# A Mamba block with an fp8 feed-forward on one core: two scalings go from VectorE to ScalarE, and the hand-written step tables of four engines get new places

## The reference, cut to what matters

```python
xz = x @ W_in + b_in;  x_in, z = split(xz)             # 256 inner channels each
x_conv = silu(conv1d(x_in, conv_w, causal, 4 taps) + conv_b)
Bm, Cm = split(x_conv @ W_xp + b_xp)                   # 16 states
delta  = softplus(x_conv @ W_dt + b_dt)
h_t = exp(delta_t * A) * h_{t-1} + (delta_t * x_t) * B_t   # per channel and state
y_t = sum_s h_t[s] * C_t[s] + D_skip * x_t
out = (y * silu(z)) @ W_out + b_out
x1  = x + layernorm(layernorm_alpha_beta(xn + out))    # xn = layernorm(x)
# feed-forward: per-tensor fp8 (e4m3) rounding of both operands
hq, wq = fake_quant_fp8(layernorm(x1)), fake_quant_fp8(weight)
out = x1 + layernorm(hq @ wq.T + bias)
```

## Time and profile before

| what | us |
|---|---|
| median of 3 runs | 593.94 (593.66 to 595.33) |
| the profiled execution | 596.42 |
| its span, first to last instruction | 594.7 |
| busy: PE / DVE / ACT / POOL | 512.0 / 502.9 / 433.9 / 351.0 |

### The profile page before, as it was taken

The page is one execution under the profiler, slowest core; times in us unless marked ns, Lnnn a source line. Parts: engine busy times, 40 slices in busy tenths (PEclk is TensorE's granted clock), DMA queues, the critical chain, the costliest instruction groups (busy, mean ns, idle before and its releaser), DMA issues.

```text
span 594.7 us, 9011 instructions
## 1 busy us (share of the span) xinstructions
PE 512.0 (86%) x2875; PEld 397.1 (67%) x2875; DVE 502.9 (85%) x1013; ACT 433.9 (73%) x870; POOL 351.0 (59%) x327
## 2 busy tenths in 40 slices
PE   6989899998899989997999889988999879765292
PEld 4557686877687767876687758676877668655030
DVE  5167699988998998889898899898789999987786
ACT  2558994999579965999399949995699958730264
POOL 3054364948577674948394858676585759530154
PEclk8989999999899889998899999998999899878555
DMA  7201633053505360434304350535042514460018
GB/s 185 63 1 23 121 69 74 11 98 72 106 2 107 62 115 2 76 62 85 64 15 94 72 107 1 106 73 107 0 89 54 107 35 81 78 127 0 1 35 196
DMA packets 19918, 41.21 MB, mean 69 GB/s; under 512 B 3744, under 2 KB 10016, under 8 KB 19872
## 3 DMA queue, kind: packets, MB, share of 16 engines
q0 software_dynamic: 9936, 34.87, 31.1%
q1 hardware_dynamic: 9936, 5.78, 3.7%
HBM read 3.68 MB, written 2.10 MB: 10 GB/s over the span
## 4 chain that ended last, share of the span: by engine, by line
PE 52%; DVE 20%; ACT 12%; POOL 8%; issue 5%; DMA 0%; DVEq 0%; POOLq 0%; ACTq 0%
PE drive L1078 16%; PE hT L1095 11%; PE fbank L1021 8%; DVE state L1301 8%; PE fbank L1036 4%; PE drive L1075 3%; DVE acc_d L1324 3%; ACT term L828 3%; POOL u L538 3%; PE fbank L1113 2%; ACT nrm L718 2%; PE drive L1021 2%; ACT L771 2%; POOL state L687 1%; PE fbank L1105 1%
## 5 line engine op out<-in xcount | busy, mean ns | idle before, releaser
L1301 DVE TENSOR_TENSOR_SCAN state<-decay,drive 128x512 f32<-128x512 f32 x256 | 297.5, 1203 | 28.2 <-ACT decay L807 12.2
L807 ACT ACTIVATE decay<-delta,a_neg 128x510 f32<-128x510 f32 x256 | 171.3, 729 | 23.8 <-DVE state L1301 22.0
L1095 PE MATMUL hT<-ident,state 128*128 128x128 f32 x1024 | 148.8, 282 | 22.2 <-DVE acc_d L1324 13.8
L1078 PE MATMUL drive<-diag,uT 128*128 128x256 f32 x640 | 165.0, 405 | 0.8 <-DVE uT L1503 0.8
L1095 PEld LDWEIGHTS hT<-ident,state 128*128 128x128 f32 x1024 | 122.9, 146 | 49.5 <-ACT term L828 16.0
L1078 PEld LDWEIGHTS drive<-diag,uT 128*128 128x128 f32 x640 | 125.5, 206 | 20.2 <-issue 3.4
L828 ACT ACTIVATE term<-hT,Ct 128x256 f32<-128x256 f32 x256 | 102.5, 483 | 4.9 <-PE hT L1095 4.9
L550 POOL TENSOR_TENSOR scaled<-uT,Bt 128x1024 f32<-128x1024 f32 x48 | 95.8, 1996 | 5.9 <-DVE uT L1503 4.2
L565 POOL TENSOR_SCALAR_AFFINE_SELECT diag<-Bt 128x512 f32<-128x512 f32 x80 | 59.1, 793 | 35.4 <-PE drive L1078 17.6
L581 POOL DMA_DIRECT2D acc<-term x64 | 61.6, 967 | 18.5 <-issue 9.5
L1324 DVE SCALAR_TENSOR_TENSOR acc_d<-hT,Ct,acc_d 128x256 f32<-128x256 f32 x160 | 66.6, 471 | 5.3 <-PE hT L1095 5.3
(11 more groups left out here) (190 smaller groups left out, 661.6 us busy)
## 6 DMA issues: line engine op xcount, KB each, us to landing
acc<-term POOLq DMA_DIRECT2D x64, 512.0 KB, 4.8
out_dram<-x_all SPq DMA_DIRECT2D x7, 256.0 KB, 3.0
x_all<-term POOLq DMA_DIRECT2D x5, 256.0 KB, 3.9
x_all<-in_L_attn_x_dram SPq DMA_DIRECT2D x2, 256.0 KB, 4.0
state<-in_L_attn_conv_w_dram SPq DMA_DIRECT2D x1, 512.0 KB, 5.9
w_in<-in_L_attn_W_in_dram SPq DMA_DIRECT2D x1, 256.0 KB, 4.7
w_dt<-in_L_attn_W_dt_dram SPq DMA_DIRECT2D x1, 256.0 KB, 4.5
out_dram<-x_all SPq DMA_DIRECT2D x2, 128.0 KB, 2.7
```

What stands on the lines that cost most here:

```text
L807: last = nc.scalar.activation(decay[:, g % DECAYS, h, :, s, 1:], delta[:, par, h, :, 1:], ACT.Exp, scale=a_neg[:, h, SG * g + s:SG * g + s ...
L1078: last = nc.tensor.matmul(dst[:, :, P * c:P * c + P], uT[:, par, TC * b + c, P * h:P * h + P], diag[:, n % DIAGS, c, :, :], start=True, st ...
L1095: last = nc.tensor.transpose(hT[:, ring(n, c), DI * s + P * h:DI * s + P * h + P], state[:, n % STATES, h, s, P * c:P * c + P], ident[:, :])
L1301: nc.vector.tensor_tensor_scan(state[:, n % STATES, h, :, :].rearrange("p s t -> p (s t)"), decay[:, g % DECAYS, h, b, :, :].rearrange("p ...
```

## The change

Four parts. (1) In the feed-forward, ScalarE scales the weight and the bias, behind its first two scalings of h; VectorE keeps the five column instructions. TensorE's first bias product waits for ScalarE's two. (2) `LEAD` is 2, not 3: at unit n GpSimd makes the factor of unit n + 2. (3) The last unit made by a product is 14, not 15. (4) Some twenty places in the four tables move, most of them by one to three.

```diff
-LEAD = 3
+LEAD = 2
-MUL_U = (2, 6, 8, 10, 12, 15)
+MUL_U = (2, 6, 8, 10, 12, 14)
-POOL_STEPS = dict(front_root=(2,), front_residual=(31,), front_u=(25,), back_gate=(9,), back_affine=(18,),
-                  back_sum=(25,), sum_states=(5,), back_root=(15, 22, 25))
-ACT_STEPS = dict(back_h2T=(47,), front_xin=(5, 9), silu_table=(21,), front_silu=(21, 22, 23), exp_table=(23,),
-                 front_norm=(12,), front_xnT=(23,), front_dt=(29, 30), front_exp=(34,), front_log=(34,),
+POOL_STEPS = dict(front_root=(5,), front_residual=(27,), front_u=(25,), back_gate=(10,), back_affine=(20,),
+                  back_sum=(25,), sum_states=(8,), back_root=(15, 22, 25))
+ACT_STEPS = dict(back_h2T=(47,), front_xin=(5, 7), silu_table=(21,), front_silu=(21, 22, 23), exp_table=(23,),
+                 front_norm=(12,), front_xnT=(23,), front_dt=(25, 30), front_exp=(34,), front_log=(34,),
...
-PE_STEPS = dict(front_in=(1, 5, 20, 22), front_transpose=(24,), front_dt=(25, 28), front_bc=(36,),
-                front_ut=(41, 44), back_y=(12, 14), back_out=(18,), back_transpose=(46,))
-DVE_STEPS = dict(front_stats=(1,), front_shift=(4,), front_low=(19,), front_bc=(25,), front_delta=(24,),
+PE_STEPS = dict(front_in=(1, 5, 20, 22), front_transpose=(23,), front_dt=(25, 27), front_bc=(36,),
+                front_ut=(39, 42), back_y=(12, 14), back_out=(18,), back_transpose=(46,))
+DVE_STEPS = dict(front_stats=(1,), front_shift=(5,), front_low=(19,), front_bc=(24,), front_delta=(23,),
...
-        XS_STEPS = 10
+        XS_STEPS = 8
...
+                if grp.v == -1:
+                    act.wait_ge(xs_step, 7)
+                    nc.scalar.activation(wqT_g[:, :], wqT[:, :], ACT.Copy, scale=units[1]).then_inc(units_ready, 1)
+                    nc.scalar.activation(bias_g[:, :], fb_r[:, :], ACT.Copy, scale=units[3]).then_inc(units_ready, 1)
...
-                    pe.wait_ge(xs_step, XS_STEPS)
+                    pe.wait_ge(units_ready, 2)
...
                 nc.vector.tensor_scalar(sg, g, s_, None, ALU.mult).then_inc(xs_step, 1)
-                nc.vector.tensor_scalar(wqT_g[:, :], wqT[:, :], g, None, ALU.mult).then_inc(xs_step, 1)
-                dve.wait_ge(xs_step, 8)
-                nc.vector.tensor_scalar(bias_g[:, :], fb_r[:, :], sg, None, ALU.mult).then_inc(xs_step, 1)
+                dve.wait_ge(xs_step, 7)
                 nc.vector.tensor_scalar(eps, sg, sg, LN_EPS, ALU.mult, ALU.mult).then_inc(xs_step, 1)
```

More of the change, by code:

```diff
@@ L385, in build_sandwich @@
         xs_step = sem("xs_step")
+        units_ready = sem("units_ready")
         t_ready = sem("t_ready")
@@ L406, in build_sandwich @@
         x_k = x_all[:, :].rearrange("p (k d) -> p k d", d=DM)
-        XS_STEPS = 10
+        XS_STEPS = 8
         B_STEPS = 8
+        units = [x_scale[:, k:k + 1] for k in range(3, 8)]
         block = ctx.enter_context(nc.Block())
@@ L1585, in to_units @@
             def to_units():
-                inverse, g, s_, sg, eps = (x_scale[:, k:k + 1] for k in range(3, 8))
+                inverse, g, s_, sg, eps = units
                 nc.vector.tensor_scalar(inverse, x_scale[:, 0:1], wq_scale[:, 0:1], 1.0 / FP8_MAX ** 2,
```

## The result

The changed kernel took 615.48 us in the median of 4 runs (612.52 to 619.03), the kernel before 593.8 us in the runs beside it (592.89 to 595.33): a ratio of 1.0365, with a 95% interval of 1.029 to 1.044. The direction was forecast, the size was not: 21.7 us were lost, not 6.6, and the time lies above the range. A few executions of the experiments lay far off the others of their kernel (853 us in run 9, with TensorE at about half its clock throughout, 1277 in run 8, 625 in run 12, 606 in run 10); the ratios leave them out.

The account below looks back on a forecast made before the run. VectorE was taken to set each slot's end. Terms of 1.4 us per slot made 8.4 in six, less 0.4 in the feed-forward; with all or no clock falls, 604.4 or 599.2, taken as 600.5 us; range 588.5 to 605.

Parts of the forecast that it names:

- Rival B: Rival from the experiments: TensorE's and GpSimd's new order, with the shorter lead, costs the time by itself; no chance given.
- variance -0.45: VectorE's variance in each of six slots: no longer held by GpSimd's masks, 0.62 becomes 0.17 us, 0.45 us gained.
- delta +0.83: VectorE's delta, moved ahead of one scan: held by GpSimd's product, 0.83 us lost in each of six slots.
- shift of piece 4 +1.0: VectorE's shift of norm piece 4: held until GpSimd's u ends, 1.0 us lost per slot, the largest single term.
- VectorE's first rounding: Feed-forward: the rounding starts when GpSimd's first sum is done, 0.05 us behind it, gaining 0.4 us.
- Nothing is held by tensor_tensor: Rival: GpSimd's f32 tensor products hold no VectorE instruction; delta and shift lose nothing, 588 to 591 us; chance 0.27.
- the rival with a free delta: Rival: holds partly covered, delta not held and the clock's falls ending; 0.8 us per slot, 595.6 us; chance 0.11.
- the second hold: Rival: GpSimd's product for unit 12 holds VectorE's shift of piece 2; 2.4 us more per slot, 615; chance 0.08.
- falls that might vanish: TensorE's drops to half clock cost 5.2 us of the profiled execution; between none and all might remain.
- The mask of unit 15: GpSimd, behind the second root: TensorE gets it at about 406, still ahead of VectorE's demand; no cost counted.

Follow-up runs that it names:

- run 9: Kernel before with only GpSimd's part of the change (lead two, unit 14 for 15, GpSimd's steps): 599.78 to 602.24 us, ratio 1.0120.
- run 8: Kernel before with only VectorE's delta, B and C at their changed steps: 597.98 us, ratio 1.0065.
- run 12: Changed kernel with unit 12's product waiting for the shift of piece 2, delta, B, C and TensorE's steps as before: 592.19 us.
- run 10: Changed kernel with GpSimd's part undone (lead three, unit 15 scaled, GpSimd's steps as before): 599.6 us, ratio 1.0092.
- run 6: Changed kernel with one wait more: GpSimd's product for unit 12 waits for VectorE's shift of piece 2; 596.53 us, ratio 1.0036.
- run 14: Changed kernel with GpSimd's product for unit 12 moved ahead of the DMA of unit 5, no wait added: 599.11 us, ratio 1.0077.
- run 1: Changed kernel with ScalarE's first front_dt at step 29 again, not 25: 613.61 us.
- run 3: Changed kernel with ScalarE's first front_dt and VectorE's delta, B and C at their old steps: 608.53 us.
- run 13: Kernel before with only GpSimd's part of the change, profiled once more with TensorE's mean clock at 0.94: 602.18 us in one execution.
- run 4: Kernel before with only ScalarE's scaling of the feed-forward's weight and bias, steps and lead unchanged: 593.22 us, ratio 0.9984.
- run 5: Changed kernel with the lead of three again and unit 15 scaled by GpSimd, not 14: 633.83 us.
- run 7: Changed kernel with unit 12's product waiting for the shift of piece 2, and delta, B and C as before: 589.5 us, ratio 0.9924.
- run 11: Changed kernel, delta, B, C as before; unit 12's product waits for piece 2's shift, unit 15's mask for piece 6's: 586.91 us, ratio 0.9885.

## Why the prediction was right in direction and wrong in size

**The bound was read rightly.** VectorE's closed row sets the slot's end: the period grew by 3.56 us for 3.8 us of holds, with TensorE waiting longer for acc_d (28.5 us in 19 waits, before 13.8 in 14). Rival B of the experiments fell with runs 6 and 14, which keep every other part of the change and lose 2.4 and 5.4 us.

**The three terms of the forecast were right as holds**: variance -0.45 (measured -0.45), delta +0.83 (+0.72), shift of piece 4 +1.0 (+0.93; the forecast's own times, 398.6 to 399.65 less the shift's 0.15, give 0.9), 1.2 us a slot for 1.4. VectorE's first rounding came 0.4 us earlier, as forecast. The Trainium skill's rule ("SBUF — State Buffer", section "SBUF: two separate sides"), by which one of VectorE and GpSimd holds a shared port pair for a whole instruction, is borne out for products of f32: 1.92 us for 1.20, delta's own work beginning about where the product ends, and 1.08 us for 0.15, ending with u. "Nothing is held by tensor_tensor", which had 0.27, is excluded. So is the rival with a free delta (0.11, 595.6): its time lies near run 6's, but delta was held in full there.

**The step that failed** is the one on the second hold: "From the traces the DMA's issue comes too late for it. Chance 0.08." The rival's mechanism and place were right. Its price was too low, 2.4 us a slot where 2.50 + 0.53 were measured, and that its 615 meets 615.48 is luck: it stands on a base of 600.5 where run 6 has 596.53. The prediction gives no times for "too late". Worked out again from the traces, an estimate: ScalarE ended unit 5's term at 382.60 in the kernel before, 0.8 us later is 383.4, and the DMA's row starts 0.6 us behind the term's end (331.49 and 332.10 in the changed kernel), so at 384.0, with the product's row 0.58 us behind it at 384.6 and the shift at 384.27. The rows came out so: DMA 0.18 us ahead of the shift, product 0.40 behind its start. The step's fault is its condition that the product must start "just before" the shift: it took for granted that a product can hold only what starts after its own row does. Runs 6 and 14 show that this was wrong: with the same starts to 0.02 us, the shift is free when the product isn't ready behind the DMA, and held to the product's end when it is. Runs 1, 3 and 13 show a second fault of that step: it asked about one instruction. Three small instructions stand there in a row (L1378, L1380, L1357), the product is longer than all three, and which of them it catches depends on 0.9 us of ScalarE's time. So the chance of a hold there was more than that of one instruction being caught.

By the same page's rule, whoever starts first keeps the pair; the trace agrees only if the start is not that of the product's row. For the shift at 332.28 the rows alone would give it the pair, and it was held.

**The clock.** The forecast took off between 0 and 5.2 us for falls that might vanish, and chose the middle. What happened is another thing: the falls are still there (0.95 in every second period) and cost nothing, 66.45 us against 66.44. Where VectorE's row is longer than TensorE's work, TensorE at half clock has room. So even without the second hold the 600.5 would have been some 4 us too high: run 6, which is the change without it, took 596.53. With the whole of the 5.2 us off, the forecast's terms give 593.94 + 8.0 - 5.2 = 596.7 us. Run 4, which keeps the slots of before, bears out that an execution near the median has nearly the same falls (periods of 63.91, 64.35, 64.37, 62.89 and 63.67 us at 592.24). But that the sum comes within 0.2 us is partly luck: in run 6 a period is 63.82 us at full clock, 0.94 more than before where its terms make 1.2, and the stretch behind the last delta is 3.4 us longer than before.

**The whole.** In the profiled executions the span grew by 22.6 us. The five periods after the second delta grew by 11.6 in all (331.20 against 319.6), since 62.88 was only one of the five before. The rest lies ahead of the second delta (5.4 us) and behind the last one (5.6 us). Ahead of it lies the first of the six long shifts of piece 2, in a period of 61.92 us for 59.77; in the period ahead of that, front_low takes 2.28 us beside a product, before 1.00; and at 30.51 a product of VectorE on two SBUF tiles takes 1.64 us for 0.69 beside one of GpSimd. Behind the last delta lie delta's own hold (1.92), a shift of piece 4 (1.08) and L1378 (1.42 for 0.16). No run separates these from the falls at both ends, which differ between the two profiled executions.

**Small terms.** The mask of unit 15 was late, as said, and TensorE waits 0.9 us for it (at 356.73), where it had no such wait before; no run shows what this costs. TensorE's moved steps cost nothing clear of noise (run 12). ScalarE's were not tried by themselves; run 10, which has them beside delta's move, loses 1.6 us more than run 8, within the intervals.

## What to carry to other kernels

When an instruction of GpSimd that reads SBUF is moved, look at every short VectorE instruction with SBUF operands within its length on either side, not at one, and count a DMA issue that stands right ahead of it on GpSimd's queue as its beginning. One semaphore wait that lets the short instruction go first can give back most of it: here 19 us of 21.7 for the product, and two such waits with delta's old place made the changed kernel 1.2% faster than the one before. A cost that a slower clock has on one engine must be dropped from the sum when another engine's row becomes the longer one.

## What the hardware showed that was not expected

- A product ready behind a DMA issue on GpSimd held a VectorE instruction that started 0.40 us ahead of the product's row, until the product's end (2.66 us for 0.16), in five slots; in the sixth, at 464.46, one that started 0.10 us ahead (2.35 us), while L1378 in that slot, from 0.09 to 0.24 us behind the DMA's start, was free. The DMA issue alone (run 14) or with a product that isn't yet free (run 6) held nothing, at the same distance of 0.18 to 0.19 us. A mask behind a DMA didn't either (run 5), with the shift starting 0.18 us after the DMA. Whether that is for the mask's own wait or for its kind was not tried.
- It isn't only instructions with two tensors: the tensor_scalar L1378, on 4 elements per partition, took 2.19 us for 0.16, and front_low, a tensor_scalar on 1024 elements, 1.21 to 2.28 us for 0.69. The reciprocal between L1378 and the shift was free at 464.24, 0.27 us behind the DMA's start and 0.32 ahead of the product's row; no run shows it beside a product in full. Not every small one is held: in the feed-forward of the changed kernel L1597 to L1603, three tensor_scalars and a reciprocal on one column, take 0.15 to 0.21 us beside GpSimd's sum of 584.32 to 585.58.
- Some orders spread more between executions than others: run 7 from 586.6 to 595.4 us and run 10 from 595.9 to 602.2 in ten executions each, run 4 from 592.2 to 594.8 in ten, run 11 from 586.5 to 587.2 in four. Why is open.
